# GpSimd's gathers released one by one by the progress of TensorE, in a block of mixture-of-experts, attention and mixture-of-experts

## The reference

```python
x = x + 0.5 * ffn(layernorm(x))      # x: (16, 256, 128) float32
x = x + attention(layernorm(x))      # 16 heads of 8, causal, softmax, projection
x = x + 0.5 * ffn(layernorm(x))      # the same weights as the first ffn
...
# ffn: 16 experts, top 2 of each token by a linear router
logits = xt @ Wg.T + bg
top_vals, top_idx = top_k(logits, 2); rw = softmax(top_vals)
gate, up = gu[..., ::2], gu[..., 1::2]          # gu = xt @ Wgu[e] + bgu[e]
gated = (clip(up, -7, 7) + 1) * min(gate, 7) * sigmoid(1.702 * min(gate, 7))
out = sum over the 2 experts of rw * (gated @ Wd[e] + bd[e])
```

## Time and profile before

| | |
|---|---|
| median of 3 runs | 847.68 us (847.01 to 850.09) |
| profiled execution: its own time, its span | 847.43 us, 845.6 us |
| mean granted clock of TensorE | 0.829 of 2.4 GHz |
| PE busy | 517.7 us (61%) |
| DVE busy | 508.3 us (60%) |
| ACT busy | 314.8 us (37%) |
| POOL busy | 333.4 us (39%) |

### The profile page before, as it was taken

The page is one execution under the profiler, slowest core; times in us unless marked ns, Lnnn a source line. Parts: engine busy times, 40 slices in busy tenths (PEclk is TensorE's granted clock), DMA queues, the critical chain, the costliest instruction groups (busy, mean ns, idle before and its releaser), DMA issues.

```text
span 845.6 us, 18950 instructions
## 1 busy us (share of the span) xinstructions
PE 517.7 (61%) x6235; PEld 351.5 (42%) x6235; DVE 508.3 (60%) x2562; ACT 314.8 (37%) x602; POOL 333.4 (39%) x332
## 2 busy tenths in 40 slices
PE   2304059978756969696969978453731899229400
PEld 2303048857523535353535545231420687118300
DVE  6727348847766757585857878544245687017822
ACT  1001038846324535353535534221211687017300
POOL 2774740052464343535252030516076002740274
PEclk9999979979869899898989989677655799559855
DMA  9911125535536070615152460101011355214332
GB/s 300 293 53 54 53 61 144 147 94 134 168 126 220 9 222 28 198 50 178 54 173 74 128 200 1 39 14 44 7 47 59 97 150 141 65 48 128 111 93 60
DMA packets 107230, 90.21 MB, mean 107 GB/s; under 512 B 11025, under 2 KB 99474, under 8 KB 106770
## 3 DMA queue, kind: packets, MB, share of 16 engines
q1 hardware_dynamic: 72850, 59.86, 22.9%
q0 software_dynamic: 8192, 16.79, 6.7%
q10 hardware_dynamic: 26112, 12.59, 5.1%
HBM read 47.25 MB, written 41.94 MB: 105 GB/s over the span
## 4 chain that ended last, share of the span: by engine, by line
PE 37%; issue 31%; DVE 13%; another core or an unknown queue 8%; POOL 4%; DMA 3%; ACT 2%; SPq 1%; ACTq 0%; DVEq 0%; POOLq 0%
PE banks L1501 11%; PE banks L1512 5%; PE banks L1489 4%; DVE by_token L772 3%; POOL by_token L483 3%; PE banks L1291 2%; PE banks L1241 2%; PE banks L1267 2%; PE banks L1216 1%; PE banks L1435 1%; PE banks L1269 1%; PE banks L1232 1%; DMA k_by_part<-k_parts 1%; PE banks L1197 1%
## 5 line engine op out<-in xcount | busy, mean ns | idle before, releaser
L772 DVE CUSTOM_DVE_ANT_0 by_token<-banks,konst_sb 128x128 f32<-128x128 f32 (+1 forms) x512 | 147.1, 353 | 64.0 <-remote 43.8
L533 POOL DMA_INDIRECT rows_by_expert<-by_token,posi x120 | 116.7, 973 | 103.8 <-DVE posi L958 69.3
L1501 PE MATMUL banks<-xT,pT 128*64 128x128 f32 x1536 | 119.8, 297 | 41.8 <-issue 31.8
L1501 PEld LDWEIGHTS banks<-xT,pT 128*64 128x64 f32 x1536 | 92.0, 147 | 65.0 <-issue 55.6
L605 ACT ACTIVATE pT<-banks 128x1536 f32<-128x1536 f32 x64 | 92.8, 1450 | 64.5 <-PE banks L1269 61.7
L483 POOL DMA_INDIRECT by_token<-results_by_tile,tilepos x64 | 60.9, 951 | 119.6 <-DMA results_by_tile<-ysb 100.7
L706 ACT ACTIVATE pT<-w_experts 128x384 f32 x192 | 90.0, 516 | 34.4 <-PE banks L1512 12.3
L483 POOL DMA_INDIRECT yg<-results_by_tile,tilepos x64 | 61.4, 959 | 70.7 <-DMA results_by_tile<-ysb 52.2
L1106 DVE SCALAR_TENSOR_TENSOR sig<-banks,sig 128x256 f32<-128x256 f32 x96 | 40.4, 421 | 80.9 <-ACT sig L716 67.4
L1512 PE MATMUL banks<-pT,gT 128*64 128x128 f32 x768 | 64.7, 287 | 7.4 <-issue 3.9
L716 ACT ACTIVATE sig<-banks 128x256 f32<-128x256 f32 x96 | 36.8, 384 | 69.5 <-remote 54.3
(11 more groups left out here) (160 smaller groups left out, 1033.2 us busy)
## 6 DMA issues: line engine op xcount, KB each, us to landing
xt<-rows_by_expert SPq DMA_DIRECT2D x192, 64.0 KB
results_by_tile<-ysb ACTq DMA_DIRECT2D x96, 128.0 KB
q_stack<-q_by_part SPq DMA_DIRECT2D x8, 1024.0 KB
k_stack<-k_by_part SPq DMA_DIRECT2D x8, 1024.0 KB
q_by_part<-q_parts SPq DMA_DIRECT2D x16, 384.0 KB, 3.2
k_by_part<-k_parts SPq DMA_DIRECT2D x16, 384.0 KB, 3.3
x_resident<-in_x SPq DMA_DIRECT2D x8, 256.0 KB, 5.4
w_experts<-in_w_gu SPq DMA_DIRECT2D x1, 2048.0 KB
```

Of the source, the lines that this page charges most:

```text
L533: pool.indirect_dma_start(out=rows_dram, out_offset=bass.IndirectOffsetOnAxis(ap=posi[:, c:c + 1], axis=0), in_=rows_of(f, q)[:, i, :], in ...
L772: last = nc.vector.tensor_tensor_reduce(masked[:, (3 * g + qt) * P:(3 * g + 2 * qt + 1) * P], of, lag, 1.0, NEG * NEG_BELOW, ALU.add, ALU. ...
L1501: last = nc.tensor.matmul(bank[2 + k % 2][h * HALF:(h + 1) * HALF, at:at + P], w_tile[:, 2 * k + i, which * F + h * HALF:which * F + (h + ...
```

## The change

Every gather of pairs 0 and 1 now waits for a value of s_y (pass 1), one per pair of expert tiles: 26 to 33 for pair 0, 34 to 37 and, behind root_of_pair(0), 40 to 43 for pair 1. Pair 2's eight wait for 48, the end of pass 1. The gathers of pairs 3 to 7 wait for values of a_st, one per attention unit from the third of the block on (8(x-1) + 2, 3, 4, 5, 6, 6, 7, 8), the first two before and the other six behind the root. In the last pass the 32 gathers of the first side wait for s_y = 76 + 2j // 3. The combination is cut in three functions that issue the same three instructions; from pair 2 on they stand between the splits of q and k of the next loop step, and so after the last gather by up to a block.

```diff
-            def gather(q, to, done):
-                for j in range(QUAD * TOPK):
+            def gather(q, to, done, those, paces=None):
+
+                for j in those:
+                    if paces is not None:
+                        pool.wait_ge(*paces[j])
...
-            def gather_pair(x):
-                if x % QSIDE == 0:
+            def gather_pair(x, those, paces):
+                if x % QSIDE == 0 and those[0] == 0:
                     stored(x // QSIDE)
-                if x > 0:
+                if x > 0 and those[0] == 0:
                     pool.wait_ge(a_comb, x)
-                gather(x, a_yg, a_got)
+                gather(x, a_yg, a_got, those, paces)
...
+            def weigh(x):
+
+                pool.wait_ge(a_got, (x + 1) * (16 * QUAD * TOPK))
+                nc.gpsimd.tensor_tensor(yg_of_token, yg_of_token, wts[:, :, x * QUAD:(x + 1) * QUAD].rearrange("p k n -> p n k").unsqueeze(3).to_broadcast([P, QUAD, TOPK, C]),
+                                        ALU.mult).then_inc(a_half, 1)
+
+            def add_result(x, k):
+
+                mine = xr[:, x * QUAD:(x + 1) * QUAD, :]
+                pool.wait_ge(a_half, 2 * x + 1 + k)
+                nc.gpsimd.tensor_tensor(mine, mine, yg_of_token[:, :, k, :], ALU.add).then_inc((a_half, a_comb)[k], 1)
...
+            def parts_of(which, x):
...
-                    gather_pair(0)
+                    every = range(QUAD * TOPK)
+                    of_first = [(s_y, PAIRS + 2 + j) for j in every]
+                    of_second = [(s_y, PAIRS + 10 + j + j // 4 * 2) for j in every]
+                    gather_pair(0, every, of_first)
                     combine(0)
+                    gather_pair(1, every[0:4], of_second)
                     root_of_pair(0)
-                    gather_pair(1)
+                    gather_pair(1, every[4:8], of_second)
                     combine(1)
                     root_of_pair(1)
-                    gather_pair(2)
-                    combine(2)
+                    gather_pair(2, every, [(s_y, 2 * PAIRS)] * len(every))
                     for x in range(1, B // 2):
-                        parts_of_pair(x)
-                        if x + 1 < B // 2:
+                        later, latest = x + 1 < B // 2, x + 2 < B // 2
+
+                        of_units = [(a_st, 8 * (x - 1) + n) for n in (2, 3, 4, 5, 6, 6, 7, 8)]
+                        if later:
+                            weigh(x + 1)
+                        parts_of(0, x)
+                        if later:
+                            add_result(x + 1, 0)
+                        parts_of(1, x)
+                        if later:
+                            add_result(x + 1, 1)
+                        if latest:
+                            gather_pair(x + 2, every[0:2], of_units)
+                        if later:
                             root_of_pair(x + 1)
-                        if x + 2 < B // 2:
-                            gather_pair(x + 2)
-                            combine(x + 2)
+                        if latest:
+                            gather_pair(x + 2, every[2:8], of_units)
...
-                        gather(q, last_results[:, q * QUAD * TOPK:(q + 1) * QUAD * TOPK, :], s_got[q])
+                        paces = [(s_y, 3 * PAIRS + 4 + (q * QUAD * TOPK + j) * 2 // 3) for j in range(QUAD * TOPK)] if q < QSIDE else None
+                        gather(q, last_results[:, q * QUAD * TOPK:(q + 1) * QUAD * TOPK, :], s_got[q], range(QUAD * TOPK), paces)
```

More of the change, by code:

```diff
@@ L485, in gather @@
                         in_=results_dram[q // QSIDE], in_offset=bass.IndirectOffsetOnAxis(ap=tilepos[:, c:c + 1], axis=0)).then_inc(done, 16)
-            def gather_pair(x):
-                if x % QSIDE == 0:
+            def gather_pair(x, those, paces):
+                if x % QSIDE == 0 and those[0] == 0:
                     stored(x // QSIDE)
-                if x > 0:
+                if x > 0 and those[0] == 0:
                     pool.wait_ge(a_comb, x)
-                gather(x, a_yg, a_got)
-            def combine(x):
[L496 to L504, removed]
+                gather(x, a_yg, a_got, those, paces)
+            yg_of_token = a_yg.rearrange("p (n k) c -> p n k c", k=TOPK)
+            def weigh(x):
[6 more added lines that the diff above has]
+                nc.gpsimd.tensor_tensor(mine, mine, yg_of_token[:, :, k, :], ALU.add).then_inc((a_half, a_comb)[k], 1)
+            def combine(x):
+                weigh(x)
+                for k in range(TOPK):
+                    add_result(x, k)
             def root_of_pair(x):
@@ L508, in root_of_pair @@
                 nc.gpsimd.tensor_tensor(a_rs[:, :], a_ve[:, :], neghalf[:, 0:QUAD], ALU.pow).then_inc(a_rstd, 1)
[L510 to L518, removed]
+            def parts_of(which, x):
+                pool.wait_ge(a_rest[which], x + 1)
+                nc.gpsimd.tensor_copy(parts[which][:, 1, :], rest[which][:, :]).then_inc(a_mid, 1)
+                pool.wait_ge(a_mid, x * 2 + (which - 1))
+                nc.gpsimd.tensor_tensor(parts[which][:, 2, :], rest[which][:, :], parts[which][:, 1, :],
+                                        ALU.subtract).then_inc(a_low[which], 1)
             for f in range(2):
```

## The result

The changed kernel takes 776.21 us (median of 4 runs, 775.49 to 777.63); the kernel before, on the same chip, 848.53 (4 runs, 847.01 to 850.09). The ratio is 0.915, 95% interval 0.9129 to 0.9170: 72.3 us faster. The forecast was 782, its range 747 to 828. A run on another chip, near the end of this document, bounds what this means: there the same change made the kernel 0.8% slower.

What follows compares the result with a forecast made beforehand. The prediction took GpSimd's dense gathers to hold up TensorE's semaphore increments, and then its issue. Attention 24.5, last pass 31.5 and pass 1 9.2 sum to 65.2; 847.4 - 65.2 = 782 us, range 747 to 828.

Steps and rivals of the forecast that it cites:

- Complete recovery: Rival, whole kernel: a gather let go at the right moment costs nothing; 745 us, chance 0.13.
- weak relief: Rival, whole kernel: two gathers released together cost like a piece of a train, 2.4 us; 824 us, chance 0.10.
- Nothing happens: Rival, whole kernel: the stall has another source than dense gathers, so spacing them gives 847 us; chance 0.06.
- slower: Rival, whole kernel: each gather blocks TensorE for its full 1.4 us wherever it stands; 866 us, chance 0.09.
- pass 1: Term for expert pass 1: paced gathers of pairs 0 and 1 gain 9.2 us (0 to 16).
- attention, five blocks: Term for attention, gathers 3 to 7: a block's gathers cost 4.3 us against 9.2, gaining 24.5 us in five.
- last pass: Term for the last expert pass: the second half's gathers start at 765.9 instead of 797.43, gaining 31.5 us.
- twin: Two gathers released together, three times per attention block; taken at 1.2 us each time, between 0.3 and 2.8.
- single: A gather released alone in attention, two per block; taken at 0.35 us, between 0 and 1.4.
- The four released together: Expert pass 1: four gathers of pair 1 let go at once, put at 2.8 us.
- The combination in three steps: Attention: the same three instructions between the splits of q and k, 3.0 us of slack, nothing on the path.
- What would show it: Signs in the new profile: attention blocks of 34 to 37 us, last-pass down projections 2.0 to 2.6 us apart.

Runs made afterwards that it cites:

- e1: The changed kernel with all releases by TensorE's progress taken out, the new order of steps kept; 847.44 us, ratio 0.9928 to the kernel before.
- p1: The changed kernel with eight back-to-back indirect GpSimd gathers added in the attention block that has none; 789.67 us, that block 42.29 us.
- e4: The changed kernel with each attention gather waiting for a short GpSimd operation instead of TensorE's progress; 771.76 us, ratio 0.9072 to the kernel before.
- e2: The changed kernel with releases kept only in attention, the expert passes' gathers back to back; 814.22 us, ratio 0.9555 to the kernel before.
- e3: The changed kernel with releases kept only in the expert passes, attention's gathers back to back; 808.24 us, ratio 0.9473 to the kernel before.
- c1: The changed kernel, unaltered, measured again on the last chip; 659.48 us, ratio 1.0076 to the kernel before on that chip.

## Why the prediction was right, point by point

**The mechanism.** Dense gathers hold TensorE back: shown, on the chips of the first two groups, by e1 (releases taken out, back to 0.9928) and p1 (a train added where there was none, 10.1 us for eight). By what way they do it is open; the rows show late increments of TensorE ("remote", 5.69 us in the earlier trace rows, 5.88 in p1). *Complete recovery* (745) and *weak relief* (824) failed on size. *Nothing happens* and *slower* failed there, and on the last chip *nothing happens* is what holds, with 5 us of loss. I had given it 0.06 from one chip's trace; none of my cases allowed that another chip might not show the stall.

**The sum, by landmarks of the two profiled executions** (847.43 - 776.36 = 71.1):

| term | predicted | measured | from |
|---|---|---|---|
| pass 1 | 9.2 | 7.8 | first exponential 249.42 to 241.58 |
| attention, five blocks | 24.5 | 34.9 | 453.79 - 249.42 = 204.37 to 411.04 - 241.58 = 169.46 |
| between the sixth block and the last pass | 0 | -2.7 | shift of 42.75 at the sixth block (453.79 to 411.04), of 40.09 at the transposes of the 31st pair from the start of pass 2 (713.54 to 673.45) |
| last pass | 31.5 | 30.9 | 33rd gather 797.43 to 726.48, a shift of 70.95, less 40.09 |

The time, 776 for 782, came out closer than the terms did, and that is luck in part: attention gave 10.4 us more than forecast, the other rows of the table 4.7 less.

*Attention* is the term that was mis-sized. I put the twin at 1.2 and the single at 0.35, 4.3 per block; it cost 1.66, the twin about 0.5 and the single, by e4, 0.1. The price of a single lay between 0 and the 1.4 of a train, and of a twin between 0.3 and 2.8; both turned out near the lower end. That a pause lets TensorE catch up before the next gather fits these prices, but no row shows it. The 0.3 I had read from the first two of each burst was closer than the price I took.

*Between*: the block without gathers takes 32.23 instead of 31.71, the one behind it 51.6 instead of 50.0. That is 2.2 of the 2.7. The 0.5 goes with the new order and not with the releases: e1, e2 and e3 have 32.20 or 32.21, and c1 32.19. The last pair's combination, which stood in the block before, now falls into this one; no run separates that. The 1.6 is hardly the change's: in the other kernels of the new order this second block takes from 50.2 (e2) to 52.9 us (e4), and 51.7 in c1.

*The last pass*: forecast 31.5, measured 30.9, and by its own steps. From the 76th increment of s_y to the 96th, 20 pairs should take 45.6 us at 2.28; the down projections that make them start at 674.75 and 721.62 (the two rows of L1535 above), 46.9 us, 2.34 each. Inside, where three gathers go to two pairs, it is 2.50, so three gathers cost 2 x (2.50 - 1.83) = 1.3 us and not 0.9; the last four steps of the pass, 713.40 to 721.62, are quicker (2.06 each), and from the end of the 96th, 722.28, to the 33rd gather it takes 4.2 us instead of 4.9. So this term too came out by two misses that cancel. GpSimd is late at the end, as said: 726.48 is set by its own 32nd gather.

*Pass 1*: predicted 9.2, measured 7.8 at the first exponential, but not by the prices of the gathers. At the last down projection of the pass (235.33 before, 225.87 after) 9.5 us are gained; 1.6 of them are gone again at the first exponential. Pair 2's train, which the prediction left "as before", now starts 1.9 us behind that down projection instead of 2.4 ahead of it, and so falls on the first scores. That would explain it, and e1, with the old place, has the old distance from down projection to exponential (14.1 us); but e2, in the old place too, has 15.3 against 15.7 after. The cause stays open.

Inside the pass: pair 0's eight cost 0.8 us (transposes from 172.04 to 185.64, seven steps of 1.83 and the 0.8) and not 2.5, the four singles behind the root nothing against c1 (203.05 to 214.00 is 10.95 us, 10.97 there) and not 1.0. The four released together cost more than the 2.8 put down. The transposes in the profile after:

```profile
192.24 0.44 PE L1512 MATMUL banks<-konst_sb,xt 128*128 128x128 f32 x2
196.49 0.44 PE L1512 MATMUL banks<-konst_sb,xt 128*128 128x128 f32 x2
203.05 0.64 PE L1512 MATMUL banks<-konst_sb,xt 128*128 128x128 f32 x2
```

With gathers at 190.00, 191.28, 192.54 and 193.79, the step to 196.49 is 4.25 us instead of 1.83, 2.4 more. The next step, to 203.05, with one gather in it (200.54), is 6.56 us. Most of that belongs to the hook, not to gathers: in it TensorE waits for xnT of VectorE's normalisation (L777), 3.08 us, and in c1, where nothing is held, the same step takes 5.78. So 0.8 us is extra, 3.2 together. GpSimd begins the root at 199.30, after 4.58 us of waiting for VectorE's a_ve (L768). VectorE was late in turn: its product of the slot before had waited 3.56 us for a sigmoid that ScalarE began at 195.78, behind 2.63 us of "remote". So the four gathers did make the root late, as forecast, though by way of TensorE and VectorE and not of GpSimd's queue.

*The combination in three steps*: 3.0 us of slack predicted. In the profile after the last add ends at 419.97 + 1.31 = 421.28 and the statistics of its pair start at 424.78, 3.5 later and 13.7 behind the block's first exponential (13.2 predicted). No row of attention has VectorE wait for an add. That the order of steps is worth nothing was wrong by 0.7% (e1): I had not seen that the root between the second and third gather cuts the train.

*What would show it* came, with three corrections. Blocks of 33.9 us are just under the 34 to 37 given. The down projections of the last pass are 2.34 apart in the mean, inside the 2.0 to 2.6, but singly from 1.7 to 3.5. And the second half's gathers stand at 726.48, not near 766: the 766 was a time of the trace before, which left out what the earlier stages gain; with the 40.09 of shift ahead of the last pass it is 766.6. The scatters still stall TensorE, from 493 us on (above).

## What to carry to other kernels

Look for instructions of an idle-looking engine that coincide with a standstill of another one, and take the price from blocks with and without them. Where GpSimd's indirect transfers hold TensorE back, they are best given a pause each: a short operation ahead of each, 1.04 us long, was enough in attention, and the wait on the bound engine's progress, which lets some out in twins, cost 0.8 us more in each block. Above all, measure such a gain on more than one chip before it is kept: the one here is 8.5% of the time on one chip, and a loss of 0.8% on another.

## What the runs showed of the hardware that I had not expected

- Chips, or the state they are in, differ in this one thing. The same kernel before takes 848.5, 854.2 and 854.5 us in three comparisons and 655.0 in a fourth, and the traces of the changed kernel on the chip of the result and on the last one have equal durations of single instructions (a gather 0.94, an exponential 1.45 us) and an equal block without gathers (32.2). What makes the difference the runs don't say, nor whether it stays with a chip.
- On the chip of the second group eight indirect gathers back to back cost TensorE 10.1 us; with 16 bytes a row instead of 512, 9.7; eight plain transfers of GpSimd nothing, eight of SyncE nothing.
- Paused by about 1.4 us each, eight cost 0.9 us together (chip of the first group); on the last chip neither paused nor dense ones cost anything that its rows show.
